# Second attention of a two-attention layer on one core: slot softmax two steps ahead, slot product turned into the column halves of the array

## What is computed

```python
s = hs @ Ws1.T @ Ws2.T + bs2                      # 64 slots for each of 16 heads
s = jnp.clip(s, -CLAMP, CLAMP).reshape(B, T, H, M).transpose(0, 2, 1, 3)
z = jax.lax.cumlogsumexp(s, axis=2)
es, enz = jnp.exp(s), jnp.exp(-z)
A = jnp.einsum('bhtd,bhjd->bhtj', q, k) * scale   # q, k after a rotation
A = jnp.where(mask, A, 0.0)
ok = enz * jnp.einsum('bhtj,bhjm->bhtm', A, es)   # the slot product
qv = jax.nn.softmax(ok, axis=-1)                  # the slot softmax
W2 = jnp.einsum('bhtm,bhjm->bhtj', qv * enz, es)
W2 = jnp.where(mask, W2, 0.0)
o = jnp.einsum('bhtj,bhjd->bhtd', W2, v)          # then RMS norm, gate, output weights
```

## Time and profile before

| | |
|---|---|
| median of 3 runs | 821.48 us (821.04 to 825.55) |
| the profiled execution, its own time | 821.59 us |
| its span, first to last instruction | 819.7 us |
| PE busy | 770.2 us, 94% |
| DVE, ACT, POOL busy | 581.3, 435.4, 285.7 us |
| mean granted TensorE clock | 0.985 |

### The profile page before, as it was taken

How to read it: one execution, slowest core, us unless ns; L and a number is a source line. 1 busy time by engine, 2 the same in 40 slices (tenths; PEclk the granted TensorE clock), 3 DMA queues, 4 the chain that set the end, 5 groups by cost and what they waited for, 6 DMA issues and landing times.

```text
span 819.7 us, 14465 instructions
## 1 busy us (share of the span) xinstructions
PE 770.2 (94%) x4556; PEld 654.7 (80%) x4556; DVE 581.3 (71%) x1502; ACT 435.4 (53%) x1188; POOL 285.7 (35%) x291
## 2 busy tenths in 40 slices
PE   5899999999999995799999999999999999999963
PEld 4788888888888883478888888888888888888852
DVE  4555555555555558878887888798879888887686
ACT  3555565555556542465556465656564665555420
POOL 6311020201102014444536346355364463553222
PEclk9999999999999999899999999999999999999997
DMA  6110101101010100100101001001010010000001
GB/s 226 40 52 13 38 13 38 51 0 51 13 38 13 51 1 14 53 0 14 54 0 54 10 13 51 0 13 51 0 33 31 13 51 0 13 0 0 1 1 52
DMA packets 23653, 23.74 MB, mean 29 GB/s; under 512 B 2369, under 2 KB 23361, under 8 KB 23506
## 3 DMA queue, kind: packets, MB, share of 16 engines
q1 hardware_dynamic: 23634, 23.51, 9.0%
HBM read 22.45 MB, written 1.05 MB: 29 GB/s over the span
## 4 chain that ended last, share of the span: by engine, by line
PE 90%; DVE 5%; POOL 1%; ACT 1%; issue 1%; DMA 1%; SPq 0%; DVEq 0%; ACTq 0%; POOLq 0%
PE ps L1276 22%; PE ps L1483 11%; PE ps L1385 7%; PE ps L1283 5%; PE ps L1306 5%; PE ps L1349 3%; PE ps L1390 3%; PE ps L1495 3%; PE ps L1520 3%; PE ps L1325 3%; PE ps L1507 2%; PE ps L1402 2%; PE ps L1537 2%; PE ps L1539 2%; PE ps L1509 2%; PE ps L1508 2%
## 5 line engine op out<-in xcount | busy, mean ns | idle before, releaser
L1276 PE MATMUL ps<-xT_hi,w_hi 128*128 128x512 f32 x256 | 110.4, 431 | 5.3 <-DVE rot L1012 3.6
L1276 PE MATMUL ps<-xT_hi,w_lo 128*128 128x512 f32 x256 | 102.0, 399 | 0.0
L1276 PE MATMUL ps<-xT_lo,w_hi 128*128 128x512 f32 x256 | 101.5, 396 | 0.0
L1042 DVE TENSOR_TENSOR wt<-ps,const 128x384 f32<-128x384 f32 x128 | 68.2, 554 | 40.4 <-PE ps L1496 20.4
L383 POOL TENSOR_TENSOR w_lo<-w_raw,w_hi 128x512 fp32r<-128x512 f32 x32 | 40.8, 1285 | 155.8 <-ACT w_hi L535 154.1
L439 POOL TENSOR_TENSOR rot_s<-rot_s,const 128x512 f32<-128x512 f32 x64 | 82.1, 1293 | 21.1 <-ACT rot_s L678 21.1
L580 ACT ACTIVATE wt<-wt,negmax 128x128 f32<-128x128 f32 (+1 forms) x128 | 56.7, 444 | 28.2 <-DVE negmax L906 28.2
L894 DVE TENSOR_TENSOR v<-ps,bv_b 128x256 f32<-128x256 f32 x64 | 27.0, 422 | 51.9 <-PE ps L1283 51.9
L697 ACT ACTIVATE v<-ps 128x256 f32<-128x256 f32 x64 | 24.5, 382 | 72.4 <-PE ps L1483 72.2
L1276 PEld LDWEIGHTS ps<-xT_hi,w_hi 128*128 128x128 f32 x256 | 49.0, 192 | 15.1 <-issue 4.5
L1031 DVE RECIPROCAL enz<-zs 128x128 f32<-128x128 f32 x64 | 60.3, 943 | 1.0 <-ACT zs L684 1.0
(11 more groups left out here) (170 smaller groups left out, 2236.9 us busy)
## 6 DMA issues: line engine op xcount, KB each, us to landing
w_raw<-a_w_q SPq DMA_DIRECT2D x8, 256.0 KB, 2.8
w_raw<-a_w_k SPq DMA_DIRECT2D x8, 256.0 KB, 3.2
wv<-a_w_v SPq DMA_DIRECT2D x8, 256.0 KB, 3.4
wo<-a_w_o SPq DMA_DIRECT2D x8, 256.0 KB, 2.7
w_raw<-b_Wq SPq DMA_DIRECT2D x8, 256.0 KB, 2.7
w_raw<-b_Wk SPq DMA_DIRECT2D x8, 256.0 KB, 3.3
wc<-b_Wv SPq DMA_DIRECT2D x8, 256.0 KB, 3.5
wc<-b_Wg SPq DMA_DIRECT2D x8, 256.0 KB, 3.7
```

The lines of the kernel that those rows point to most:

```text
L1042: d.tensor_tensor(dst, src[:, 0:384], tri3, ALU.mult).then_inc(done, 1)
L1276: ins = mm(PJ[n[0]], w[:, m, c, h * P:(h + 1) * P], x[:, c, cols], start=(t == 0), stop=(t == len(terms) - 1))
```

## The change

Two things are changed, both in the second attention.

The slot product is turned. `es` becomes the stationary operand (64 columns for a head) and `wt` the moving one; the result is transposed, slots by tokens, and the two heads are written to the two halves of the partitions of `X_qt`, by the two column halves of the array. ACT copies it to `okT`, two PE transposes turn it back into `X_ok`.

The slot softmax runs a step further ahead (the first two pieces of the diff are of PE and ACT, the next two of PE's `b_body`, the last of PE ahead of the loop). In step x the scores, the slot product and the softmax are now those of x + 2, the transposes of `qp` (`b_slot_transpose`) and the copy into `zT` (`b_z_copy`) are those of x + 1 and stand ahead of the o product. Tasks move with it: even steps now carry c0 to c3 and et, odd steps carry s, q0, q1, z, k0, k1, the first half pair of tasks is done ahead of the loop, and the last three steps have none. Within the steps, k0 now stands between z and the slot product; on DVE `b_rope_cos` of q0 and q1 stand ahead of `b_recip` and `b_gated`; on POOL one `rope_mul` stands ahead of `rms`.

```diff
             def b_ok(x, b, phase):
...
                 for h in range(2):
                     own = slice(h * M, (h + 1) * M)
-                    mm(X_ok[:, h, 0, :], wt[:, h, 0:P], es[:, 2 * b, own], start=True, stop=True)
-                    mm(X_ok[:, h, 1, :], wt[:, h, P:T], es[:, 2 * b, own], start=True, stop=False)
-                    ins = mm(X_ok[:, h, 1, :], wt[:, h, T:T + P], es[:, 2 * b + 1, own], start=False, stop=True)
+                    mm(X_qt[own, :], es[:, 2 * b, own], wt[:, h, 0:T], start=True, stop=False)
+                for h in range(2):
+                    own = slice(h * M, (h + 1) * M)
+                    ins = mm(X_qt[own, P:T], es[:, 2 * b + 1, own], wt[:, h, T:T + P], start=False, stop=True)
+                ins.then_inc(b_okT_ps, 1)
+
+            def b_ok_transpose(x):
+
+                pe.wait_ge(b_okT, x + 1)
+                for t in range(2):
+                    ins = tr(X_[0][:, t * P:(t + 1) * P], okT[:, t * P:(t + 1) * P], ident)
                 ins.then_inc(b_okps, 1)
...
+            def b_ok_copy(x):
+
+                act.wait_ge(b_okT_ps, x + 1)
+                s.activation(okT[:, :], X_qt, ACT.Copy).then_inc(b_okT, 1)
...
+                    ti, tb = (i, b + 1) if b < B - 1 else (i + 1, 0)
+                    rest = not (last and b >= 1)
+                    nxt = not (last and b >= 2)
...
+                        if not (last and b == B - 1):
+                            b_slot_transpose(x + b + 1)
                         b_o_product(x, b, i, last)
                         if nxt:
-                            b_scores(x + b + 1, (b + 1) % B, 2 * i + (b + 1) // 2)
-                        if rest:
-                            b_task(i, 1 + b // 2, B_TASKS.index("c2"), half, phase)
+                            b_scores(x + b + 2, (b + 2) % B, 2 * i + (b + 2) // 2)
+                        if rest:
+                            b_task(ti, 1 + tb // 2, B_TASKS.index("c2"), half, phase)
                         if nxt:
-                            b_ok(x + b + 1, (b + 1) % B, 2 * i + (b + 1) // 2)
+                            b_ok(x + b + 2, (b + 2) % B, 2 * i + (b + 2) // 2)
...
+            b_scores(1, 1, 0)
+            b_slot_transpose(0)
+            b_task(0, 1, B_TASKS.index("s"), 1, 1)
+            b_task(0, 1, B_TASKS.index("q0"), 1, 1)
+            b_task(0, 1, B_TASKS.index("q1"), 1, 1)
+            b_ok(1, 1, 0)
+            b_task(0, 1, B_TASKS.index("z"), 1, 1)
             pe.wait_ge(s1_done, 4)
+            b_ok_transpose(1)
+            b_task(0, 1, B_TASKS.index("k0"), 1, 1)
+            b_task(0, 1, B_TASKS.index("k1"), 1, 1)
```

More of the change, by code:

```diff
@@ L739, in b_body @@
                             t("q1")
+                        if b == 1 and not last:
+                            s.activation(wo_hi[:, :, :], wo[:, :, :], ACT.Copy, scale=gwh[:, 0:1]).then_inc(b_.wo_hi, 1)
+                        if rest:
                             t("z")
+                        if last and b == 3:
+                            ffn_copy(1, 1)
+                        if nxt:
+                            b_ok_copy(x + b + 2)
                         act.wait_ge(b_ogt_ps, x + b + 1)
@@ L781, in b_body @@
                         if nxt:
-                            b_okexp_step(x + b + 1)
+                            b_okexp_step(x + b + 2)
+                        if last and b == 2:
+                            ffn_copy(1, 0)
             act.wait_ge(init_done, 3)
@@ L1082, in b_body @@
                 for b in range(B):
-                    rest = not (last and b >= 2)
-                    first = b % 2 == 0
-                    half = 1 - b // 2
-                    phase = 2 * i + 1 + b // 2
-                    nxt = not (last and b == B - 1)
-                    def n(j):
-                        return (*slot(i, 1 + b // 2, j), slot_ps(i, 1 + b // 2, j))
-                    if first:
-                        b_gate(slot(i, b // 2, NB - 1), phase - 1, 3, b // 2)
+                    ti, tb = (i, b + 1) if b < B - 1 else (i + 1, 0)
@@ new lines, in b_body, with n @@
+                    rest = not (last and b >= 1)
+                    nxt = not (last and b >= 2)
+                    half = 1 - tb // 2
+                    phase = 2 * ti + 1 + tb // 2
+                    def n(name):
+                        j = B_TASKS.index(name)
+                        return (*slot(ti, 1 + tb // 2, j), slot_ps(ti, 1 + tb // 2, j))
+                    if b % 2 == 1:
+                        if not (last and b == 3):
+                            b_gate(slot(ti, tb // 2, NB - 1), phase - 1, 3, tb // 2)
@@ L1545, in b_body @@
                 for b in range(B):
-                    rest = not (last and b >= 2)
-                    half = 1 - b // 2
-                    phase = 2 * i + 1 + b // 2
-                    nxt = not (last and b == B - 1)
-                    c3_bank = slot(i, 1 + b // 2, NB - 1)[0]
-                    if b % 2 == 0:
-                        pe.wait_ge(b_qp, x + b + 1)
-                        for t in range(2):
-                            ins = tr(X_qt[:, t * P:(t + 1) * P], qp[:, t, :], ident)
-                        ins.then_inc(b_qt_ps, 1)
+                    ti, tb = (i, b + 1) if b < B - 1 else (i + 1, 0)
```

357 lines of the change are left out of this document (201 added, 156 removed).

## The result

Slower, by about one per cent: median 831.04 us (830.91 to 832.86, 4 runs) against 821.75 (821.04 to 825.55) of the kernel before, a ratio of 1.0109 with a 95% interval of 1.0075 to 1.0143. The forecast was 833.0 with a range of 819 to 846. The profiled execution took 830.98 with a span of 829.2, so 9.5 more than the span of before (819.7), and its mean granted clock was 0.975 against 0.985.

The account below looks back on a forecast made before the run. TensorE sets the pace, DVE next at 83%. Loop +2.5, ahead of it +5.0, behind the tasks +4.1, last filled step +0.3, four products outside -0.4: +11.5 on 821.59, 833 us, range 819 to 846.

Parts of the forecast that it names:

- The turned product: Slot product of each step, es stationary: 0.95 us with its pause, 1.90 a cycle, a change of -0.76.
- Loads exposed: Rival: the slot products' weight loads don't overlap matmuls, about 35 more than non-overlapping halves, 880 us; chance 0.02.
- The gate chain in the c step: Steps with c tasks: squares, inverse root and gate finish 5.25 after the o product starts, so PE waits 0.26.
- The pause ahead of the loop: Before the second attention's loop: PE waits 3.0 for batch 1's mask on DVE, then slow clock costs 1.6.
- The steps without tasks: After the tasks end: three such steps instead of two, idle 16.7, +4.1; 33 from last c3 to last og transposes.
- The copy wait in the q step: Steps with q tasks: okT copy path takes 0.79 from product's end, og transposes cover 0.44, PE waits 0.35.
- The copy behind og in the c step: Steps with c tasks: okT copy ends at 5.78, og transposes at 5.69, so PE waits 0.09 more.
- VectorE's slack: In the loop: DVE's queue has about 0.2 left at its tightest place, the W2 masks of the c step.
- DVE binds: Rival: in the loop DVE's 0.2 is gone, o waits for W2 masks, 0.6 a cycle, 841 us; chance 0.06.
- The whole cycle: Two steps of the second attention: -0.76 + 0.44 + 0.35 + 0.35 - 0.2 = +0.18, so 27.8 us; +2.5 over 14.
- W2, which no longer waits for zT: In the loop: W2's wait of 0.16 for zT goes, with just-in-time transposes behind qp, saving 0.2 a cycle.
- Why og waits 4.4 in the last step but one: Second step without tasks: og wait put at 4.3, because DVE quantizes before it gates.

Follow-up runs that it names:

- three short moves: Changed kernel with et transposes before og transposes, last c3 task in the first unfilled step, batch 1's scores mask earlier on VectorE: 821.46 us, ratio 0.9982 to the kernel before.

## Why the prediction was right, and where it was off

**Right, and shown.**
- *The turned product*, forecast at 0.95 with its pause: 0.89. Its gain is 2.66 - 2 x 0.89 = 0.88 a cycle, where 0.76 stood. The run without overlap shows that it is the two halves that bring it. The Trainium skill ("TensorEngine Tiling (Array Packing)", Key Properties) says that a change of the tiling mode drains the engine and that tiles run in parallel; the 0.32 instead of 0.23 at 534.07 and the 0.80 against 1.44 agree.
- *Loads exposed* (the rule that I weighed against the change): none. Even with both heads in one column half, where the row groups and the columns are the same, the product took 1.35 (554.02 to 555.37, the last start plus the 0.22 of its kind), as the o product with the same columns does (1.34). The Trainium skill ("TensorE: Matmul & The Clock Gate", Part 3) has a weight load overlap only where its row group differs; the measurement decides against it. The same Part, under "The mechanism", also has loads pulled ahead when they go to the background weight buffer, and with that sentence the measurement agrees.
- *The gate chain in the c step*: og 5.25 behind the o product forecast, 5.36 measured, a wait of 0.26 forecast, 0.32 measured from start to start (0.25 in the bracket). The run with the et transposes ahead of it confirms that this wait is real time.
- *The pause ahead of the loop*, 3.0 forecast, 3.05 measured, with the clock at 0.62 in the 4.4 behind it; 4.5 went with it when the mask came first, against 4.6 forecast for pause and clock.
- *The steps without tasks*: forecast 33 from the last c3 to the last transposes of og, 34.2 measured (window from 775.24). Waits for masks (0.91 and 1.02) and og (4.42 and 3.76) stand where they were laid out; the first two were put at 1.6 each and the last at 3.3, and these misses partly cancel.

**Off in size.**
- *The copy wait in the q step*, 0.35 forecast, 0.11 measured. The step that failed is the 0.79 from the end of the product to PE's next work. The copy started 0.12 behind the first transposes of og and PE went on 0.43 after that, 0.55 in all. Both rows of the zT copy had more in them than the copy. Its start was read as 0.38 after the last transpose started; the row gives their end as 511.79 + 0.44 = 512.23, and the copy follows 0.04 later, as that of okT follows 0.05 after the end of the product (534.55 + 0.39 = 534.94). And the 0.52 to W2 is 0.09 longer than the 0.43 to the transposes of okT: that is the size of the pause with which a product in row halves begins, though no run separates the two.
- *The copy behind og in the c step*, 0.09 forecast, 0.05 measured.
- *VectorE's slack*, 0.2 forecast. It was gone in one of two c steps, in six of seven behind the 0.43 that DVE stands at the turn of the loop: 0.30 of wait, 0.15 a cycle in the mean. My layout of DVE's queue had no price for the turn of the loop. The rival "DVE binds" had its place right and its size too high: it needed 0.6 a cycle. A wait of that size came only when the masks were moved, and then for the keys, behind an addition that ran beside GpSimd.
- *The whole cycle*: -0.88 + 0.42 (transposes) + 0.11 + 0.32 + 0.05 + 0.15 and -0.15 for W2, which no longer waits for zT, make +0.02 where +0.18 stood; measured +0.01. That they meet so closely is in part luck: shifts of 0.1 to 0.2 that are in no term, such as 0.12 that PE no longer stands between z and the product and 0.10 more at the output products of the q step, cancel. Over 14 cycles that is the 2.4 by which 833 was too high.
- *Why og waits 4.4 in the last step but one*: put down to quantizing; that is 0.6 of it, the chain alone is 3.8. The number was right and the cause wrong.

**What stays open.** Of the 9.4 at the ends, 4.5 is the pause with its clock and 1.0 is clock behind the last transposes of og. The 3.9 that is left belongs, by the forecast's account, mostly to the third step without tasks, waits and slow clock together, and no run splits it: the mean clock is 0.975 against 0.985, and how much of this the third step brings and how much differs from run to run can't be told apart here. For the same reason the medians of the runs with two steps ahead, with the mask first and with the filled tail are trusted less than the landmarks in their traces.

## What to carry to other kernels

Software pipelining by one more step costs at both ends what it saves in the middle: count the steps that get no filler, at their chains' full length and at the clock that follows a wait, and the start, where the new first product may stand behind work that isn't urgent; here 9.4 of ends stood against a loop that was level. When a product gets shorter, look at the chain beside it that was just hidden, and put work that depends on nothing (here four transposes) between the product and the wait: it gave 0.31 a cycle back. Then measure each end by itself: three short moves took the change from 1.1% slower to level.

## What the runs showed of the hardware

- Two f32 products with 64 output columns each, in the two column halves of the array: 0.80 together against 1.44 one after the other in the same half, both up to the next block, 1.8 times, with a pause of 0.09 on entering the form. With the same columns streamed, 64 output columns in one half take as long as 128 (1.35 against 1.34).
- VectorE stood 0.43 without a releaser (540.95) each of the six times its queue came round the loop, with the loop's branch in that stretch, and not where the code is written out: in a queue without slack that is a wait of TensorE.
- A wait of 3.05 ahead of the loop was followed by 4.4 at a mean granted clock of 0.62, and behind the wait of 4.42 in the tail the output projections took 2.05 instead of 1.10.
- Order on VectorE can be worth more than its work: two adjacent pieces swapped, with the same instructions, cost 0.46 a cycle (27.57 to 28.03), 6.4 in the loop.
- An addition of two tiles on VectorE that takes 0.69 took 1.33 and 1.77 where it started beside a GpSimd product of 1.29, and ended 0.55 after it both times. The other way round it shows too: in the changed kernel GpSimd's product takes 1.50 in the six steps where it starts during that addition (541.29), and 1.30 at 569.04.
